# Splitting each low-weight subtraction between VectorE and GpSimd, normalising rows on ScalarE, and moving side work to other slots

## What is computed

```
xn  = layernorm(x)
s   = attention(xn): layernorm * norm_g; q = xn Wq (8 heads of 64), k and v from Wkv (one shared head);
      q, k l2-normalised and scaled; softmax(q k^T) v; times Wout; layernorm * out_norm_g
g   = silu(moe(xn)): 8 experts, top 2, capacity 2560 rows an expert, gelu(x w1 + b1) w2 + b2, weighted by the gates
out = x + s * g
```

## Time and profile before

| | us |
|---|---|
| median of 3 runs | 3018.44 (3018.26 to 3020.81) |
| the profiled execution | 3019.07 |
| its span, first to last instruction | 3017.3 |

### The profile page before, as it was taken

The page is one execution under the profiler, slowest core; times in us unless marked ns, Lnnn a source line. Parts: engine busy times, 40 slices in busy tenths (PEclk is TensorE's granted clock), DMA queues, the critical chain, the costliest instruction groups (busy, mean ns, idle before and its releaser), DMA issues.

```text
span 3017.3 us, 86339 instructions
## 1 busy us (share of the span) xinstructions
PE 2790.6 (92%) x38277; PEld 1846.0 (61%) x38277; DVE 2054.7 (68%) x2889; ACT 1874.5 (62%) x2371; POOL 999.1 (33%) x664
## 2 busy tenths in 40 slices
PE   5899999989989989999999999999888999998996
PEld 3556666656655656767666666766555655555564
DVE  6787877889867863334333433358888988888885
ACT  5666666666656665556565656457666666666664
POOL 3333323313866310000000000025555656556544
PEclk8999999999999999999999999999999999999997
DMA  2212222002432001211212221110111111111101
GB/s 95 97 61 101 83 86 99 33 27 75 142 107 97 22 31 55 72 65 63 86 60 69 72 81 48 40 35 28 46 40 54 51 42 45 44 41 45 35 23 45
DMA packets 111015, 184.13 MB, mean 61 GB/s; under 512 B 12649, under 2 KB 78129, under 8 KB 110641
## 3 DMA queue, kind: packets, MB, share of 16 engines
q1 hardware_dynamic: 98352, 145.04, 14.5%
q0 software_dynamic: 12288, 33.57, 3.3%
HBM read 92.58 MB, written 85.98 MB: 59 GB/s over the span
## 4 chain that ended last, share of the span: by engine, by line
PE 67%; DVE 15%; issue 8%; ACT 7%; POOL 2%; DMA 0%; another core or an unknown queue 0%; SPq 0%; DVEq 0%; ACTq 0%; POOLq 0%
PE pair L609 16%; PE bank L686 14%; PE pair L672 14%; DVE arena L1181 7%; PE bank L631 5%; PE bank L636 5%; PE bank L629 5%; ACT arena L834 5%; PE bank L548 3%; PE bank L590 2%; PE bank L656 1%; DVE q_n L1102 1%; ACT oT L722 1%; POOL arena L1300 1%; DVE c_work L1144 1%
## 5 line engine op out<-in xcount | busy, mean ns | idle before, releaser
L1181 DVE TENSOR_TENSOR arena<-arena 128x1024 bf16<-128x1024 f32 (+1 forms) x860 | 1117.0, 1315 | 311.5 <-ACT arena L834 300.4
L834 ACT ACTIVATE arena<-pair 128x1024 f32<-128x1024 f32 (+1 forms) x1032 | 1014.2, 1015 | 368.8 <-PE pair L609 345.5
L609 PE MATMUL pair<-qT,kT 128*128 128x512 f16 (+1 forms) x4096 | 899.5, 389 | 83.3 <-ACT arena L834 79.3
L629 PE MATMUL bank<-vhl,arena 128*128 128x65 bf16 x8192 | 778.0, 194 | 37.7 <-POOL arena L1300 22.9
L631 PE MATMUL bank<-vhl,arena 128*128 128x64 bf16 x8192 | 778.9, 196 | 6.2 <-issue 6.1
L629 PEld LDWEIGHTS bank<-vhl,arena 128*128 128x128 bf16 x8192 | 609.6, 100 | 99.6 <-POOL arena L1300 26.5
L631 PEld LDWEIGHTS bank<-vhl,arena 128*128 128x128 bf16 x8192 | 593.2, 98 | 57.2 <-issue 7.9
L636 PE MATMUL bank<-vhl,arena 128*128 128x65 bf16 x8192 | 590.4, 195 | 5.2 <-issue 5.0
L1300 POOL TENSOR_TENSOR arena<-arena 128x1024 bf16<-128x1024 f32 (+1 forms) x172 | 349.6, 2033 | 612.8 <-ACT arena L834 612.3
L609 PEld LDWEIGHTS pair<-qT,kT 128*128 128x128 f16 (+1 forms) x4096 | 201.5, 96 | 546.9 <-issue 428.6
L1230 POOL TENSOR_TENSOR q_small<-q_small,minus_half 128x8 f32<-128x8 f32 x64 | 126.8, 1981 | 1058.6 <-DVE q_small L1098 1058.0
(11 more groups left out here) (192 smaller groups left out, 2427.4 us busy)
## 6 DMA issues: line engine op xcount, KB each, us to landing
routed_rows<-h_f SPq DMA_DIRECT2D x80, 256.0 KB, 4.5
att<-routed_rows SPq DMA_DIRECT2D x40, 512.0 KB, 4.4
expert_rows<-att SPq DMA_DIRECT2D x40, 512.0 KB, 2.9
raw<-in_L_ffn_w SPq DMA_DIRECT2D x32, 512.0 KB
xn_rows<-s_hl SPq DMA_DIRECT2D x16, 512.0 KB, 3.1
xT_out<-xn_rows SPq DMA_DIRECT2D x64, 128.0 KB
w_lo<-in_L_attn_x SPq DMA_DIRECT2D x64, 128.0 KB
out<-w_lo SPq DMA_DIRECT2D x64, 128.0 KB
```

The costliest lines, as they stand in the source:

```text
L609: t = nc.tensor.matmul(into, kT[g // BG % 2][rows, part, keys], qT[g % 2][rows, h, :], start=(turn == 0), stop=(turn == 1))
L629: nc.tensor.matmul(bank[:, at:at + DH + 1], p_top[:, s, cols, 1], V[:, kb, 0:DH + 1], start=(kb == 0 and qb == 0), stop=False, skip_group_ ...
L834: nc.scalar.activation(p_f32[:, n % NP, columns(n)], pairs[n % 2][:, columns(n)], ACT.Exp).then_inc(exped, 1)
L1181: nc.vector.tensor_tensor(p_lo[:, n % NP, c], p_f32[:, n % NP, c], p_top[:, n % NP, c, 1], ALU.subtract).then_inc(lowed, 1)
```

## The change

- The subtraction of each step is cut by columns: of 1024, VectorE takes the first 640 (5/8) and GpSimd the other 384, in every step outside the 172 slots of routing and scatter, where VectorE still takes all. `on_pool` is gone.
- `weigh` waits for the exponent, makes the 16 products of the high weights, and waits only then for both parts of the low ones.
- ScalarE normalises the rows (Identity with a scale and a bias per partition); VectorE makes the bias, -mean times the reciprocal deviation, in one small instruction (`shift`). For groups 4 and up the four row statistics and the four normalisations are divided over two slots.
- `statistics`, `prepare_kv`, `prepare_q` and `project_out` stand in other slots: the query projection 3 slots later, the key and value projection 2 earlier, the output chain 2 earlier with its transposes 3 slots (not 4) and its projection 8 (not 7) behind its start. That sets when the side bank is used.
- The two routing matmuls take a bank each in turn, the second 3 slots after the first.

The core of the diff; the rest replaces the constants by their lists:

```diff
 NP = 5
 LAG = 3
 BEHIND = 4
-S_TURN = 9
-K_TURN = 9
 Q_TURN = 11
-O_TURN = 4
-O_PROJECT = 7
-POOL_EVERY = 5
 
 
 class Queue:
...
-    KV_AT += [base[g - BG] + 38 for g in range(BG, NG)]
-    Q_AT = [S_TURN + 3 + 6 * j for j in range(GT)]
+    S_AT = [3 * g for g in range(BG)] + [base[0] + 24 * (g - BG) for g in range(BG, NG)]
+
+    S_SHIFT, S_NORM, S_HI, S_LO, S_TURN, S_HALF, S_LOGITS = [
+        [early] * BG + [late] * (NG - BG) for early, late in ((3, 5), (4, 7), (5, 9), (6, 11), (9, 13), (1, 2), (3, 4))]
+    KV_AT = [12 + 6 * g for g in range(BG)]
+    KV_AT += [base[g - BG] + 36 for g in range(BG, NG)]
+    K_TURN = [9] * BG + [8] * (NG - BG)
+    Q_AT = [12 + 6 * j for j in range(GT)]
     for t in range(GT, NT):
-        Q_AT.append(base[t // GT - 1] + 16 * (t % GT))
+        Q_AT.append(base[t // GT - 1] + 16 * (t % GT) + 3)
     O_AT = []
     for t in range(NT):
         g, j = divmod(t, GT)
         if g == XG:
             O_AT.append(experts_at + 1 + 5 * j)
         elif g + 1 < NG:
-            O_AT.append(base[g + 1] + 16 * j + 10)
+            O_AT.append(base[g + 1] + 16 * j + 8)
         else:
             O_AT.append(place["post", 0, 0] + 1 + 6 * j)
+    O_TURN = [3 if t // GT not in (XG, NG - 1) else 4 for t in range(NT)]
+    O_PROJECT = [8 if t // GT not in (XG, NG - 1) else 7 for t in range(NT)]
     C_AT = [base[XG + 1] + 20 + 13 * t if t < EARLY else O_AT[t] + 9 for t in range(NT)]
     C_ORDER = sorted(range(NT), key=lambda t: C_AT[t])
...
     C_SEQ = {t: i for i, t in enumerate(C_ORDER)}
-    R_AT = S_AT[-1] + S_TURN + 6
+    R_AT = S_AT[-1] + S_TURN[-1] + 6
     SCATTER_AT = R_AT + 44
     W_AT = [R_AT + 46, R_AT + 62] + [place["hidden", NQ * (e - 1), 0] + 14 for e in range(2, E)]
-
-    def on_pool(n):
-        return n % POOL_EVERY == POOL_EVERY - 1 and not R_AT <= place["scores", n] < SCATTER_AT + 2 * NT
-
...
         return slice(active[0] * BANK, (active[-1] + 1) * BANK)
+
+
+    shared = [not R_AT <= place["scores", n] < SCATTER_AT + 2 * NT for n in range(NSTEP)]
+    shared_to = np.cumsum(shared).tolist()
+
+    def shares(n):
+        c = columns(n)
+        middle = c.start + (c.stop - c.start) * 5 // 8 if shared[n] else c.stop
+        return slice(c.start, middle), slice(middle, c.stop)
 
...
-                bank, free = side.take(routed, N_ROUTE["counted"])
-                where["route"] = bank
-                if free:
-                    pe.wait_ge(*free)
-                pe.wait_ge(dve_const, 4)
-                pe.wait_ge(routed, N_ROUTE["mask"])
-                nc.tensor.matmul(bank[:, :], onesb[:, :], mask16, start=True, stop=True).then_inc(route_counted, 1)
-                pe.wait_ge(routed, N_ROUTE["total"])
-                nc.tensor.matmul(bank[:, :], upto[:, :], mask16, start=True, stop=True).then_inc(route_counted, 1)
+                for k, (kind, weights) in enumerate((("total", onesb), ("counted", upto))):
+                    yield from clock.at(R_AT + 20 + 3 * k)
+                    bank, free = side.take(routed, N_ROUTE[kind])
+                    where["route", k] = bank
+                    if free:
+                        pe.wait_ge(*free)
+                    pe.wait_ge(dve_const, 4)
+                    pe.wait_ge(routed, N_ROUTE["mask"])
+                    nc.tensor.matmul(bank[:, :], weights[:, :], mask16, start=True, stop=True
+                                     ).then_inc(route_counted, 1)
...
@@ -630,6 +632,11 @@
                                          start=(kb == 0 and qb == 0), stop=False, skip_group_check=True)
                         nc.tensor.matmul(bank[:, at:at + DH], p_top[:, s, cols, 1], V[:, kb, DH + 1:VW],
                                          start=False, stop=False, skip_group_check=True)
+                pe.wait_ge(lowed, n + 1)
+                if shared[n]:
+                    pe.wait_ge(lowed_pool, shared_to[n])
+                for i, g, h, kb in halves(n):
+                    V, bank = vhl[g // BG % 2], acc_banks[(g * H + h) % 3]
                     for qb in range(GT):
                         at = qb * (DH + 1)
...
-                yield from clock.at(S_AT[g] + 4)
+                xs = x_of(g)
+                yield from clock.at(S_AT[g] + S_NORM[g])
+                act.wait_ge(s_shift, g + 1)
+                for j in range(GT):
+                    if j == 2 and g >= BG:
+                        yield
+                    nc.scalar.activation(xs[:, j, :], xs[:, j, :], ACT.Identity, scale=rstd[:, g, 0, j:j + 1],
+                                         bias=shift[:, j:j + 1]).then_inc(s_normed, 1)
+                yield from clock.at(S_AT[g] + S_HI[g])
                 act.wait_ge(s_normed, GT * (g + 1))
                 act.wait_ge(s_turned, 2 * (g - 1))
                 act.wait_ge(s_stored[i], 16 * (g // 2))
                 cast(s_hl[i][:, :, 0, :], x_of(g)[:, :, :]).then_inc(s_hi, 1)
...
                 for j in range(GT):
+                    if j == 2 and g >= BG:
+                        yield
                     nc.vector.bn_stats(bn_s[:, j, :], xs[:, j, :]).then_inc(s_stat, 1)
+                if g >= BG:
+                    yield
                 for j in range(GT):
                     dve.wait_ge(s_stat, GT * g + j + 1)
                     nc.vector.bn_aggr(mean1[:, g * GT + j, :], bn_s[:, j, :]).then_inc(s_aggr, 1)
...
                 dve.wait_ge(s_rstd, g + 1)
-                for j in range(GT):
-                    nc.vector.tensor_scalar(xs[:, j, :], xs[:, j, :], mean1[:, g * GT + j, 0:1],
-                                            rstd[:, g, 0, j:j + 1], ALU.subtract, ALU.mult).then_inc(s_normed, 1)
-                yield from clock.at(S_AT[g] + 5)
+                dve.wait_ge(s_normed, GT * g)
+                nc.vector.scalar_tensor_tensor(out=shift[:, :], in0=mean1[:, g * GT:(g + 1) * GT, 0], scalar=-1.0,
+                                               in1=rstd[:, g, 0, :], op0=ALU.mult, op1=ALU.mult).then_inc(s_shift, 1)
+                yield from clock.at(S_AT[g] + S_LO[g])
                 dve.wait_ge(s_hi, g + 1)
                 nc.vector.tensor_tensor(s_hl[g % 2][:, :, 1, :], xs[:, :, :], s_hl[g % 2][:, :, 0, :],
                                         ALU.subtract).then_inc(s_lo, 1)
-                yield from clock.at(S_AT[g] + S_TURN + 3)
+                yield from clock.at(S_AT[g] + S_TURN[g] + S_LOGITS[g])
                 dve.wait_ge(s_scored, g + 1)
                 nc.vector.tensor_reduce(logits[:, g * GT:(g + 1) * GT, :], where["logits", g][:, 0:GT * 3 * E].rearrange(
...
                 yield from clock.at(R_AT + 20)
-                bank = where["route"]
                 dve.wait_ge(route_counted, 1)
-                v(nc.vector.tensor_copy(total, bank[:, :].rearrange("p (t e) -> p t e", e=E)), "total")
+                v(nc.vector.tensor_copy(total, where["route", 0][:, :].rearrange("p (t e) -> p t e", e=E)), "total")
+                yield from clock.at(R_AT + 23)
                 dve.wait_ge(route_counted, 2)
-                v(nc.vector.tensor_copy(row, bank[:, :].rearrange("p (t e) -> p t e", e=E)), "counted")
+                v(nc.vector.tensor_copy(row, where["route", 1][:, :].rearrange("p (t e) -> p t e", e=E)), "counted")
                 yield
                 a, b, reach = total, scan_a, 1
                 while reach < NT:
...
@@ -1177,7 +1196,7 @@
             def low(n):
                 dve.wait_ge(exped, n + 1)
                 dve.wait_ge(weighed, n - NP + 1)
-                c = columns(n)
+                c, _ = shares(n)
                 nc.vector.tensor_tensor(p_lo[:, n % NP, c], p_f32[:, n % NP, c], p_top[:, n % NP, c, 1],
                                         ALU.subtract).then_inc(lowed, 1)
 
...
             def statistics(g):
-                yield from clock.at(S_AT[g])
+                yield from clock.at(S_AT[g] + (3 if g >= BG else 0))
...
@@ -1296,12 +1315,12 @@
             def low(n):
                 pool.wait_ge(exped, n + 1)
                 pool.wait_ge(weighed, n - NP + 1)
-                c = columns(n)
+                _, c = shares(n)
                 nc.gpsimd.tensor_tensor(p_lo[:, n % NP, c], p_f32[:, n % NP, c], p_top[:, n % NP, c, 1],
                                         ALU.subtract).then_inc(lowed_pool, 1)
 
             def main(kind, a, b):
-                if kind == "att" and a is not None and on_pool(a):
+                if kind == "att" and a is not None and shared[a]:
                     low(a)
 
             clock.run(slots, main, [constants()] + [statistics(g) for g in reversed(range(NG))] + [route()] + [
```

More of the change, by code:

```diff
@@ L450, in statistics @@
                 for half in range(2):
-                    yield from clock.at(S_AT[g] + S_TURN + half)
+                    yield from clock.at(S_AT[g] + S_TURN[g] + S_HALF[g] * half)
                     bank, free = side.take(s_turned_copied, 2 * g + half + 1)
@@ L1201, in main @@
                 if kind == "att":
```

(2 more changed lines are left out.)

38 lines of the change are left out of this document (16 added, 22 removed).

## The result

The changed kernel takes 3037.74 us (median of five, 3033.94 to 3050.35) against 3018.26 (3014.79 to 3020.81): 1.0073 of the time before, 95% interval 1.0049 to 1.0096. It is slower, on the other side from the forecast of 2995 us and inside the range. The profiled execution took 3033.94 us, the fastest of the five, with a span of 3032.2, 14.9 us more than before.

A forecast was written before the change was run, and what follows sets the result against it. The prediction took TensorE as the bound, with its waits and the clock they cost as what could be won. Its terms summed to -23 us on the profiled 3019.07, giving a forecast of 2995 us, range 2940 to 3050.

The forecast's parts named there:

- The middle wait of `weigh`: One more TensorE wait a step, between high and low products: +3 us, bounds 0 to 15.
- then for up to 0.8 us in each: Shared subtraction: GpSimd blocks VectorE up to 0.8 us in every step, instead of up to 1.9 in one of five.
- I take it as even: Late stage, 390 steps: VectorE gives back 66 us of work and may take back up to 164 in waits; judged even.
- late waits for GpSimd, +12: TensorE's waits for GpSimd behind the experts, where GpSimd's load grows: +12 us, bounds -15 to +50.
- Output chain, -6: Query and output projections three slots apart on one bank, not one: 6 us won with clock, bounds -12 to +5.
- Exponents, -10: ScalarE waits less for `q_n`, so TensorE's 79.3 us of waits for the exponent shrink: -10 us, bounds -30 to +20.
- Start, -2: At the start, four normalisations leave VectorE, for which TensorE waits: -2 us, bounds -5 to 0.
- Norm, 0: Normalising moved to ScalarE, in the start and first 288 steps, covered by scores and products: 0 us, bounds -8 to +8.
- Early waits for GpSimd, -12: TensorE's waits for GpSimd up to 665 us, 10.4 us plus clock: 12 us won back, bounds -18 to +5.
- The first: Rival: GpSimd and the exclusion become the late bound, each GpSimd subtraction waiting 0.55 us; 3037 us, chance 0.28.
- evenness is worth more: Rival: long blocks set most of 205 us of waits and clock, and a third goes; 2950 us, chance 0.15.
- ScalarE is the late one: Rival: each of 32 ScalarE tile pairs delays an exponent by up to 0.5 us uncovered; 3034 us, chance 0.05.

The follow-up runs named there:

- e3: The changed kernel, but each fifth step's subtraction whole on GpSimd and the others whole on VectorE; 0.9941 of the kernel before.
- e1: The kernel before with only the new order in `weigh` (high products before the wait for low weights); 0.9989 of the kernel before.
- e2: The kernel before with the new order in `weigh` and the shared subtraction, in the old slots; 1.0245 of the kernel before.
- e4: The changed kernel with the output chain started one slot earlier and TensorE's slots left in place; 1.0028 of the kernel before.
- e7: The changed kernel with the output chain started one slot earlier and every subtraction whole on VectorE; 0.9616 of the kernel before.
- e8: The changed kernel, but GpSimd writes zeros to its 384 columns and reads nothing, leaving out their low weights; 0.9492 of the kernel before.

## The prediction against the runs

**Right.** TensorE is the bound and its waits the price. Two subtractions exclude each other: VectorE's whole pieces are 0.80 us at the shortest and GpSimd's 0.815, as worked out, and their means are 1.09 and 1.17. Waits for GpSimd ahead of the experts are gone, the routing wait is gone, the clock there is 0.98, late waits for GpSimd number 24, the experts are unchanged. The middle wait of `weigh` costs nothing (+3 forecast). One of the signs didn't come: GpSimd is busy 80% between 2030 and 2800 us, not over 85%. For slots I had -8 in the routing and -16 for output chain and exponents; 11 us came in the routing stretch and 19 (e3 against e1, with the norm's new place) in the first 283 steps.

**The step that failed** is "then for up to 0.8 us in each". I bounded VectorE's wait by one GpSimd piece because in the earlier trace rows it waited for one. With one GpSimd subtraction in five steps there never were two ready in a row. With one in each step they queue up behind two gathers, and VectorE waits for the whole queue: 5.89 us. "I take it as even" rests on the same step. In the mean it was nearly so: behind the experts a whole step took VectorE 1.375 us before, four fifths of which are 1.10 a step, and its piece takes 1.179 after. The long blocks are what was left out, and with them the term for late waits for GpSimd, +12, came to 48 to 59. The evidence was in reach. The longest in the earlier trace rows, 3.99 us, is 2.77 above VectorE's own 1.22 and more than one GpSimd piece of 1.91. The kernel before, VectorE and then GpSimd, at that moment:

```profile
2726.20 3.99 DVE L1181 TENSOR_TENSOR arena<-arena 128x1024 bf16<-128x1024 f32 x1
```

```profile
2725.11 1.39 POOL L1286 DMA_INDIRECT w_lo<-expert_rows,gather_from  x1 [0.30 <-issue]
2726.52 0.73 POOL L1293 TENSOR_TENSOR w_lo<-c_work,w_lo 128x256 f32<-128x256 f32 x1
2727.20 1.89 POOL L1300 TENSOR_TENSOR arena<-arena 128x1024 bf16<-128x1024 f32 x1
```

Two instructions behind a gather, back to back, and VectorE waits for both: the same queue, two long instead of seven.

**Terms of the wrong size.** *Late waits for GpSimd, +12:* the whole late loss by the shares is 48 us (e3) to 59 (e2), at or over my upper end of +50. In the old slots the late waits for GpSimd itself grow by 47.5 us (e2 against e1). In the changed kernel these rose by 15.4 us only; the division came as well (9.8, from nothing), and the late wait for `o_rest` (37.1) is as large in e3 and so not the shares' doing. The clock, which I had put at 9 us there, took no more than before in the changed kernel. *Output chain, -6:* the wrong sign. I counted the bank's distance and not that transposes now follow their start by one slot less, with VectorE late: 8.5 us became 71.0. e4 measures the slot, 10 us ahead of the experts. *Exponents, -10:* the wait did fall, from 79.3 to 38.2, and behind the experts (50.0 to 31.7) no time came of it, since TensorE was held elsewhere: e4 brings it back to 54.0 over the whole span, 44.9 late, when `o_rest` falls. *Start, -2:* the first exponent came 1.1 us later. *Norm, 0:* +13 in the kernel before, outside my bound of +8, though with four tiles in a slot where the forecast had two; each tile is 0.094 us dearer than taken. *Early waits for GpSimd, -12:* the waits are gone, but sharing gives 3.5 us (e3 against after, on two chips) or costs 4 (e2 against e1, on one) in the first 283 steps; the blocks that VectorE meets in each step probably take the rest back (e7, without them, is 12 us shorter there than e4, on another chip).

**The rivals.** The first gave 3037, and 3037.74 was measured, but its working was not what happened: it wanted GpSimd to wait 0.55 us for each piece and to be over 85% busy. Its pieces average 1.09 us late, 0.28 above the shortest, and it is busy 617.7 of 770 us, 80%. With 0.28 us for each its own formula gives 591 + 390 x 0.28 = 700 of 770 us, no loss at all. GpSimd did not run out of time; it was late and blocked others in clusters. So it had the stage and the engines right and the mechanism wrong. That the totals agree is partly chance: late it priced +44, 8 of it as clock at GpSimd's pieces, and 46 came without that clock; for all the rest it had -25, and -31 came ahead of the experts. That evenness is worth more (2950) is refuted by e3 and e2. That ScalarE is the late one is too: its waits, not its work, grew, `qhl` for `q_n` from 57.3 to 93.9 us. What no rival held is that GpSimd should subtract nothing: 2904.63 us.

The Trainium skill, page SBUF — State Buffer, section Summary: rules for kernel authors, says that the later of the two waits for the whole of the earlier. The traces agree for one against one (1.49 us at the longest with pauses), and show besides that for a VectorE instruction "the earlier" can be all that GpSimd has ready.

## What to carry to other kernels

Before sharing element-wise work of VectorE with GpSimd, add the two durations instead of taking the larger, and then look at what is queued ahead of GpSimd's pieces: the wait can be as long as the row of instructions that is ready, not one of them. Read the longest of a group, not only its mean, and ask which other engine ran at that moment. And measure the version without any sharing first: here an engine at 90% with even steps beat one at 85% with help by 2.3% to 2.4%.

## What the runs showed of the hardware

- Back-to-back GpSimd instructions kept a VectorE subtraction out through seven of them, 5.89 us for 0.80 of work. A wait on GpSimd's own signal ahead of each piece let VectorE in (longest 1.49 us). The other way round no trace shows such a block: GpSimd's longest piece in the changed kernel is 1.80 us for 0.82 of work.
- Gathers issued by GpSimd did not block VectorE: in e7, with gathers and no subtraction on GpSimd, 1016 of VectorE's whole steps took 1.236 us on average, longest 1.76:

```profile
L1206 DVE TENSOR_TENSOR arena<-arena 128x1024 bf16<-128x1024 f32 x1016 | 1226.1, 1236 | 208.5 <-ACT arena L855 179.2 <-issue 16.9 <-PE bank L649 9.3
```

- GpSimd's writes alone hardly lengthened VectorE's piece of 640 columns: in e8 it took 0.828 us on average, in the changed kernel 1.094.
- GpSimd's small powers (128x8, two inputs in SBUF, about 1.9 us) did not keep VectorE's subtractions out for their length: in e7, of 50 whole steps that VectorE started early enough to end within a power, none took over 1.23 us.
- The kernel before took 2990.86 us on one chip and 3018 on another. In e1's trace most of the difference to before lies in the routing stretch (339.4 against 364.7 us). Its cause stays open.
